# Scatters into the first sorted array without a bounds check

## What is computed

```python
def gnn(seq, graph, e_weight, Wx, Wh, b):
    beta = einsum('bld,du->blu', seq, e_weight) / maximum(sum(graph, 2), EPS)[:, :, None]
    agg = einsum('blu,blm->bmu', beta, graph)
    h = tanh(agg[:, t] @ Wx + h @ Wh + b)            # for t = 0 .. 127, h starts at 0
    return all h

def ffn(x, gate_w, gate_b, w1, b1, w2, b2, gamma, beta):
    vals, idx = top_k(x @ gate_w + gate_b, 2)
    w = softmax(vals)
    expert_out[e] = relu(x @ w1[e] + b1[e]) @ w2[e] + b2[e]
    y = x + sum over the two chosen experts of w * expert_out
    return layernorm(y) * gamma + beta

x = x + gnn(layernorm(x), adj, ...)
x = x + ffn(layernorm(x), ...)
```

## Time and profile before

| | |
|---|---|
| median of 3 runs | 715.17 us (713.19 to 716.28) |
| profiled execution | 712.58 us, its span 710.7 us |
| TensorE busy | 545.0 us (77%) |
| VectorE busy | 523.0 us (74%) |
| ScalarE busy | 376.8 us (53%) |
| GpSimd busy | 500.3 us (70%) |
| mean granted TensorE clock | 0.884 of full speed |

### The profile page before, as it was taken

How to read it: one execution, slowest core, us unless ns; L and a number is a source line. 1 busy time by engine, 2 the same in 40 slices (tenths; PEclk the granted TensorE clock), 3 DMA queues, 4 the chain that set the end, 5 groups by cost and what they waited for, 6 DMA issues and landing times.

```text
span 710.7 us, 17699 instructions
## 1 busy us (share of the span) xinstructions
PE 545.0 (77%) x4140; PEld 486.8 (68%) x4140; DVE 523.0 (74%) x2695; ACT 376.8 (53%) x1185; POOL 500.3 (70%) x557
## 2 busy tenths in 40 slices
PE   2666897988888872399999999900799999999920
PEld 1555575765666661299999999900799999999920
DVE  5996697887877775188888888700299899999850
ACT  2999443333333320266666666500588888888810
POOL 3677568888888887167777777776067777777774
PEclk9999999898988955599999999955699999999975
DMA  8999469322323213369876665441997676664110
GB/s 244 273 283 304 127 217 258 103 81 89 92 88 94 73 49 114 76 191 324 282 244 207 198 198 179 154 152 28 302 318 223 192 219 203 197 210 143 46 51 7
DMA packets 115094, 121.37 MB, mean 171 GB/s; under 512 B 19017, under 2 KB 99613, under 8 KB 115008
## 3 DMA queue, kind: packets, MB, share of 16 engines
q1 hardware_dynamic: 95936, 76.79, 37.7%
q0 software_dynamic: 17920, 43.03, 16.7%
q10 hardware_dynamic: 1152, 0.56, 0.3%
HBM read 68.67 MB, written 55.90 MB: 175 GB/s over the span
## 4 chain that ended last, share of the span: by engine, by line
PE 38%; ACT 7%; POOL 7%; issue 4%; DMA 1%; DVE 1%; SPq 0%; POOLq 0%; ACTq 0%; DVEq 0%
PE bank L931 19%; PE bank L947 15%; ACT hs L999 5%; POOL rows_by_second L212 4%; POOL out_dram L212 3%; PE bank L920 3%; ACT xT L980 2%; PE bank L944 2%; DMA R<-rows_by_second 0%; DMA rows_by_second<-R 0%; DMA R<-rows_by_first 0%; ACT wr L988 0%; SPq L856 0%; ACT L1008 0%; SPq L858 0%
## 5 line engine op out<-in xcount | busy, mean ns | idle before, releaser
L212 POOL DMA_INDIRECT out_dram<-R x144 | 143.2, 995 | 67.5 <-issue 39.0
L212 POOL DMA_INDIRECT rows_by_second<-R x144 | 144.7, 1005 | 62.3 <-issue 35.1
L947 PE MATMUL bank<-W,hs 128*128 x1152 | 176.8, 290 | 0.0
L999 ACT ACTIVATE hs<-bank,wr 128x128 f32<-128x128 f32 x432 | 127.1, 366 | 87.6 <-PE bank L931 81.8
L931 PE MATMUL bank<-xT,wr 128*128 128x128 f32 x1152 | 158.9, 282 | 7.1 <-ACT xT L980 7.1
L947 PEld LDWEIGHTS bank<-W,hs 128*128 128x128 f32 x1152 | 152.4, 193 | 3.8 <-issue 0.2
L931 PEld LDWEIGHTS bank<-xT,wr 128*128 128x128 f32 x1152 | 143.1, 196 | 14.4 <-ACT xT L980 14.4
L212 POOL DMA_INDIRECT rows_by_first<-st x128 | 126.7, 989 | 35.7 <-issue 33.8
L1068 DVE SCALAR_TENSOR_TENSOR R<-bank,R 128x128 f32<-128x128 f32 x288 | 87.3, 344 | 66.2 <-PE bank L947 62.7
L988 ACT COPY wr<-W1b 128x258 f32 x288 | 104.9, 426 | 17.1 <-PEq L802 17.0
L537 ACT ACTIVATE HT<-bank,bcol 128x128 f32<-128x128 f32 x128 | 46.7, 364 | 95.2 <-PE bank L450 93.9
(11 more groups left out here) (132 smaller groups left out, 856.9 us busy)
## 6 DMA issues: line engine op xcount, KB each, us to landing
R<-rows_by_second SPq DMA_DIRECT2D x144, 196.0 KB
R<-rows_by_first SPq DMA_DIRECT2D x144, 68.0 KB
xq<-in_x_dram SPq DMA_DIRECT2D x32, 256.0 KB, 3.6
aq<-in_adj_dram SPq DMA_DIRECT2D x32, 256.0 KB, 4.2
x2r<-in_x_dram SPq DMA_DIRECT2D x32, 256.0 KB, 2.8
rows_by_second<-filler SPq DMA_DIRECT2D x1, 3136.0 KB, 13.2
rows_by_second<-filler SPq DMA_DIRECT2D x16, 196.0 KB
rows_by_second<-R POOLq DMA_INDIRECT x144
```

What stands on the lines that cost most here:

```text
L212: return nc.gpsimd.indirect_dma_start(dst, bass.IndirectOffsetOnAxis(ap=idx, axis=0), src, None, bounds_check=limit[n], oob_is_err=False)
L947: i = mm(o, hs[:, h, c, k * P:(k + 1) * P], W2[:, bass.ds(e[k], 1), c, :].rearrange("p o f -> p (o f)"), start=False, stop=c == 1, skip_gr ...
L999: i = a(hs[:, h, c, k * P:(k + 1) * P], ps_h[c][h][:, k * P:(k + 1) * P], ACT.Relu, bias=wr[:, u % 2, 2 * h + k, F + c:F + c + 1])
```

## The change

The four scatters of `send` no longer go through the helper. They are issued with the same source, the same row numbers and the same destination, but without the register that holds the limit and with the default treatment of numbers beyond the end. The scatters of the expert stage are as they were, and so is everything else: on every engine the same instructions stand in the same order.

```diff
                 for j in range(QUAD):
-                    scatter(dram_a.ap(), st[:, u, j, C_POS1:C_POS1 + 1].bitcast(I32), st[:, u, j, :],
-                            ROWS).then_inc(s_sct[u], 16)
+                    g.indirect_dma_start(dram_a.ap(), bass.IndirectOffsetOnAxis(
+                        ap=st[:, u, j, C_POS1:C_POS1 + 1].bitcast(I32), axis=0), st[:, u, j, :],
+                        None).then_inc(s_sct[u], 16)
```

## The result

| | before | changed |
|---|---|---|
| median | 715.05 us (712.77 to 716.28, 7 runs) | 718.40 us (717.13 to 721.12, 7 runs) |
| ratio | 1 | 1.005, 95% interval 1.0029 to 1.0072 |
| profiled execution | 712.58 us, span 710.7 us | 721.12 us, span 719.2 us |

The changed kernel is slower by 3.35 us, where 1.5 us faster was forecast. The time lies inside the stated range, at its upper end, and the sign is wrong.

What follows compares the result with a forecast made beforehand. GpSimd was taken to bound the recurrent stage, ahead of VectorE and TensorE. 128 scatters saving 12 ns each gave 1.5 us, nothing changing afterwards: 715.17 - 1.5 = 713.7 us, range 698 to 720.

Steps and rivals of the forecast that it cites:

- GpSimd sets the pace: Recurrent stage: GpSimd bounds it, with about 1.07 us a quad to win before VectorE takes over.
- The price of the check, 12 ns: Each scatter into the first array: time saved by dropping the limit, 12 ns of 972.
- The split of the 12 ns: Price in one scatter: about 1 ns for comparing 128 numbers, 11 ns for the register holding the limit.
- 128 x d: Recurrent stage: all 128 scatters save the price of one check, d, taken as 12 ns; 1.5 us in all.
- An earlier start of the expert stage is passed on whole: After the recurrent stage: its gain reaches the end neither grown nor eaten; no stage afterwards changes length.
- these scatters keep the check: Expert stage: scatters of the first pass stay checked, and nothing after the recurrent stage changes its length.
- The loop row by row: Check inside each scatter handles 128 numbers singly, 127 ns; dropping it saves 16.3 us, 698.9 us; chance 0.33.
- That the change does nothing: First array's scatters: the default compares in the same code, d is 0, time 715.2 us; chance 0.2 of 0.55.
- The slow rival: First array's scatters: the form without a limit takes other code, 127 ns longer, 16.3 us more, 731.4 us; chance 0.12.
- The reading that therefore nothing saved on the engine could show: Scatters on GpSimd: by the skill page descriptor generation is small, so the sum would be 0; the prediction disagreed.

Runs made afterwards that it cites:

- e4: Kernel before, its 128 scatters into the first array keeping the limit but with default treatment of numbers beyond the end; 716.02 us, ratio 1.0007.
- e8: The changed kernel run again without an edit, its third run; 718.16 us, ratio 1.0024 to the kernel before.
- e7: Changed kernel, but the first quad's four scatters keep the check and the other 124 lose it; 718.20 us, ratio 1.0033 to the kernel before.
- e9: Kernel before with the first 116 scatters into the first array unchecked, the last twelve checked; 891.15 us, ratio 0.9992.
- e11: Kernel before with only the last twelve scatters into the first array unchecked; 889.13 us, ratio 0.9975.
- e15: Kernel before with only every fourth quad of the recurrent stage checked, rows of twelve unchecked scatters between; 909.80 us, ratio 1.0005.
- e5: Kernel before with only the first quad's four scatters unchecked; 909.75 us, ratio 0.9999.
- e3: Kernel before with each quad's second and fourth scatter into the first array unchecked, first and third checked; 715.19 us, ratio 0.9987.
- e10: Kernel before with each quad's first scatter into the first array checked, the other three unchecked; 891.35 us, ratio 0.9987.
- e6: Kernel before with only the last quad's four scatters into the first array unchecked; 911.38 us, ratio 1.0013.
- e13: Kernel before with only the last eight scatters into the first array unchecked; 909.13 us, ratio 0.9996.
- e17: The kernel of e10 run again; 713.84 us, ratio 0.9986 to the kernel before.

## Why the prediction was wrong, point by point

*GpSimd sets the pace.* Right, and more than I used: it is the bound in the expert stage as well. In the second pass before, 703.5 + 0.97 - 517.7 = 186.8 us are 144 scatters at 143.2 us and 143 gaps of 0.305 us. After, the pass takes 712.0 + 0.98 - 523.1 = 189.9 us: the growth of the scatters is passed on whole. The first pass before is of the same make: 492.8 + 0.97 - 305.5 = 188.3 us, of which 144.7 us are scatters.

*The price of the check, 12 ns.* Right in size: 14 ns by the median (958 after 972). e4 shows that it is the limit. The split of the 12 ns into 1 for the comparison and 11 for the register, taken from another operation and another engine, is not tested, so that the size came out may be luck.

*128 x d.* Slightly too much. The scatter behind the `pow` takes 1034 to 1039 ns and gains at most 5 ns, so busy time fell by 1.4 us and not by 128 x 14 = 1.8 us. The span of the scatters fell by 1.3 us.

*"An earlier start of the expert stage is passed on whole", "these scatters keep the check".* This is the step that failed. I took it that an untouched instruction keeps its length, put 0 for the expert stage, and had no rival for it. It measured +5.4 us of busy time in the profiled pair, 3.5 us of it the shifted median, where the first array gave back 1.4 us. With 0 in place of that term the forecast was 1.5 us faster; 3.35 us slower was measured, and e8 gives 2.5 us slower again. That 718.40 us still lies in the range, and within the 0.5% that had a chance of 0.55, is luck: the upper end was set by a rival that did not happen.

*The rivals.* The loop row by row (0.33) falls, with 14 ns in place of 127. That the change does nothing falls, too, by the same number. The slow rival got the sign, but its mechanism was wrong: the form without a limit is not longer but shorter; it is the other form that grows. The condition it gave, a median above 1000 ns in the first array, was not met.

*The pages.* The Trainium skill ("DMA: Bandwidth & Descriptors", "Anatomy of one DMA — SWDGE (gpsimd) path") takes descriptor generation as small beside the landing. That is said of the latency of one DMA. The reading that therefore nothing saved on the engine could show does not hold for scatters that follow each other: 14 ns less in each instruction gave 1.3 us in the stage, and 12 ns more in the median of the 288 came with a kernel 3.35 us slower.

*What stays open.* It is shown that the checked form takes 978 to 985 ns, in place of 972, to the end of the execution, behind a row of twelve or more unchecked scatters (e7, e9, e11, e15) and behind four at the start (e5); that rows of one, three, four or eight behind checked ones do not do it (e3, e10, e6, e13). Whether the length of the row decides, or an unchecked scatter directly behind a `pow`, is open, since both go together in these runs. In the expert stage there are two steps of length as well: medians of 983 to 985 ns where no checked scatter comes directly behind a `pow` after the first unchecked ones (the changed kernel, e7, e11), 978 to 982 where some do (e5, e9, e15). What GpSimd keeps between the instructions is not shown by any row of a profile. That it is code that has to be found again is a guess. If it is the row, I also can't say whether its count or its time decides.

## What to carry to other kernels

Where one engine is busy without a gap, price an edit over all instructions of that kind on it, those that the diff doesn't touch too: here 14 ns less in 128 of them came with 12 ns more in 288. Compare the medians of untouched groups first when a result has the wrong sign; that is where the time was. And when one form of an instruction is replaced by a leaner one at some places only, look whether the other form is still used behind them; keeping the old form at the first scatter of every quad kept the gain here and avoided the loss (e10, e17).

## What the runs showed of the hardware that I had not expected

- An indirect scatter of 128 rows with a limit takes 972 ns on GpSimd; it takes 978 to 985 ns for hundreds of instructions after twelve or more without a limit in a row (e11), and the last eight without one do nothing (e13). Only the twelve begin directly behind a `pow`, so the count is not shown to be the cause.
- Without a limit it takes 958 ns. Alternating with checked ones it stays near that (959), while the checked ones between take 977 to 981 (e3).
- The 0.30 us between two scatters and the 0.19 to 0.20 us behind a `pow` are the same with and without a limit.
- Dropping rows costs and saves nothing (0.97 us for scatters that move 0.00 MB), and neither do rows of 512 against 1568 bytes.
- In the pass into the output about one scatter in fifteen takes 1.25 us with the others at 972 ns (before, e3, e4, e17), and one in eleven takes 1.44 us with the others at 983 ns (after, e7, e8).
